# The FFN's output bias: from two TensorE matmuls per pass to an in-place GpSimd add on the residual

## What is computed

```
x = x + attn_a(layernorm(x))
x = x + ffn(layernorm(x))
x = x + attn_b(layernorm(x))
x = x + ffn(layernorm(x))
...
h = relu(x @ Wq1.T + b1)      # Wq1, Wq2: weights rounded to -1, 0, 1
out = h @ Wq2.T + b2
```

## Time and profile before

| | |
|---|---|
| median of three runs | 3095.37 us (3094.39 to 3095.38) |
| span of the profiled execution | 3093.2 us; it gives no other time of its own, so 2.2 us lie around the span |
| instructions | 79316 |
| matmul instructions | 27332, of which 128 at L446 |
| granted TensorE clock over the span | 0.988 of 2.4 GHz |

### The profile page before, as it was taken

The page is one execution under the profiler, slowest core; times in us unless marked ns, Lnnn a source line. Parts: engine busy times, 40 slices in busy tenths (PEclk is TensorE's granted clock), DMA queues, the critical chain, the costliest instruction groups (busy, mean ns, idle before and its releaser), DMA issues. The chain is left out here.

```text
span 3093.2 us, 79316 instructions
## 1 busy us (share of the span) xinstructions
PE 2935.6 (95%) x27332; PEld 2329.8 (75%) x27332; DVE 2363.1 (76%) x5980; ACT 1845.7 (60%) x3717; POOL 461.7 (15%) x1048
## 2 busy tenths in 40 slices
PE   5799999999999999999999999999999999999987
PEld 4677777777777777777777777777777777777765
DVE  5677788777788777788777788777788777888754
ACT  2356665566665566665566665566665566665565
POOL 4111111111111111111111111011111011111010
PEclk8999999999999999999999999999999999999998
DMA  2000000000000000000000000000000000000000
GB/s 65 8 11 17 16 16 3 14 16 16 16 16 3 14 16 16 16 16 3 14 16 16 16 16 3 14 16 16 16 16 3 14 16 16 16 16 3 15 11 17
DMA packets 42116, 44.86 MB, mean 15 GB/s; under 512 B 2640, under 2 KB 41424, under 8 KB 42064
## 3 DMA queue, kind: packets, MB, share of 16 engines
q1 hardware_dynamic: 42064, 44.20, 4.7%
HBM read 21.12 MB, written 16.78 MB: 12 GB/s over the span
## 5 line engine op out<-in xcount | busy, mean ns | idle before, releaser
L981 ACT ACTIVATE f_r<-HID,b1c 128x512 f32<-128x512 f32 x512 | 352.3, 688 | 501.0 <-PE HID L430 499.1
L450 PE MATMUL Y<-w2t,f_hh 128*128 128x256 f32 x2048 | 549.4, 301 | 4.8 <-DVE f_hl L1322 4.8
L450 PE MATMUL Y<-w2t,f_hl 128*128 128x256 f32 x2048 | 512.1, 283 | 0.0
L1322 DVE TENSOR_TENSOR f_hl<-f_r,f_hh 128x512 fp32r<-128x512 f32 x512 | 352.6, 689 | 127.9 <-ACT f_hh L982 119.6
L430 PE MATMUL HID<-ff_xh,w1t 128*128 128x512 f32 x1024 | 432.3, 422 | 4.6 <-DVE ff_xl L1314 4.6
L450 PEld LDWEIGHTS Y<-w2t,f_hh 128*128 128x128 f32 x2048 | 389.0, 190 | 47.9 <-issue 28.5
L430 PE MATMUL HID<-ff_xl,w1t 128*128 128x512 f32 x1024 | 406.9, 397 | 0.0
L450 PEld LDWEIGHTS Y<-w2t,f_hl 128*128 128x128 f32 x2048 | 391.0, 191 | 3.1
L982 ACT ACTIVATE f_hh<-HID,b1c 128x512 fp32r<-128x512 f32 x512 | 350.5, 685 | 0.0
L1428 DVE TENSOR_TENSOR a_s<-Q,cst 128x512 f32<-128x512 f32 x384 | 249.1, 684 | 52.1 <-PE Q L576 52.1
L1159 ACT ACTIVATE a_qz<-Q 128x512 f32<-128x512 f32 x512 | 280.0, 611 | 1.6 <-PE Q L780 1.6
(11 more groups left out here) (193 smaller groups left out, 7314.2 us busy)
## 6 DMA issues: line engine op xcount, KB each, us to landing
x<-in_x SPq DMA_DIRECT2D x32, 512.0 KB, 4.3
out<-x SPq DMA_DIRECT2D x32, 512.0 KB, 3.0
b_vm<-b_v SPq DMA_DIRECT2D x64, 96.0 KB, 2.1
x<-in_w SPq DMA_DIRECT2D x2, 512.0 KB, 4.0
a_s<-in_w_qkv SPq DMA_DIRECT2D x1, 768.0 KB, 5.0
ff_xn<-in_w SPq DMA_DIRECT2D x1, 512.0 KB, 6.7
f_r<-in_w SPq DMA_DIRECT2D x1, 512.0 KB, 7.0
cst<-in_const SPq DMA_DIRECT2D x1, 389.0 KB, 5.5
```

Source lines behind the costliest of these rows:

```text
L450: mm = pe.matmul(Y[t // 2][:, (t % 2) * D:(t % 2 + 1) * D], h[:, fb % 2, t * P:(t + 1) * P], w2t[:, fb, :], start=False, stop=(fb == FB - ...
L981: act.activation(f_r[:, fb % 2, :], banks[fb % 2][:], ACT.Relu, bias=b1c[:, fb:fb + 1]).then_inc(f_rr, 1)
L1322: dve.tensor_tensor(f_hl[:, fb % 2, :], f_r[:, fb % 2, :], f_hh[:, fb % 2, :], ALU.subtract).then_inc(f_lo, 1)
```

## The change

The bias is added to the residual tile itself, by POOL, once `normed` says that DVE has read all four tiles for the norm. `f_finish` gets one more wait, on the new semaphore. The two matmuls go, and with them their operands; the first product in each bank opens it.

```diff
-        b2f = sb("b2f", [4 * BR, D])
-        b2r = sb("b2r", [4 * BR, 2, D], F32R)
+        b2f = sb("b2f", [P, D])
...
-                    for j, y in enumerate(Y):
-
-                        rows = slice(2 * BR * j, 2 * BR * j + 2 * BR)
-                        pe.matmul(y[:], share[rows, :], b2r[rows].rearrange("p t n -> p (t n)"), start=True, stop=False,
-                                  skip_group_check=True)
                 for t in tiles:
                     for j, h in enumerate((f_hh, f_hl)):
                         mm = pe.matmul(Y[t // 2][:, (t % 2) * D:(t % 2 + 1) * D], h[:, fb % 2, t * P:(t + 1) * P],
-                                       w2t[:, fb, :], start=False, stop=(fb == FB - 1 and j == 1), skip_group_check=True)
+                                       w2t[:, fb, :], start=(fb == 0 and t % 2 == 0 and j == 0), stop=(fb == FB - 1 and j == 1),
+                                       skip_group_check=True)
...
                     dve.wait_ge(f_w2, (turn + 1) * FB)
+                    dve.wait_ge(f_biased, turn + 1)
...
+            def add_bias(turn, src):
+
+                pool.wait_ge(ff.normed, (turn + 1) * NT)
+                pool.tensor_tensor(src[:], src[:], b2f[:].unsqueeze(1).broadcast_to([P, NT, D]), ALU.add).then_inc(f_biased, 1)
```

DVE's three preparations of `b2r` and `share` go too. In POOL's order the add for `x3` stands at the head of `phase1`, before the norm of attention b. The add for `x1` stands in `phase2` behind `sines(3)`, before the norms for the next sequence:

```diff
                     sines(0)
                     sines(1)
                     own_rstd()
                     sines(2)
                     sines(3)
+                    own_bias()
                     next_rstd()
                     second_rstd()
```

More of the change, by code:

```diff
@@ L45 @@
 MASKED = -1e30
-BR = 32
 ROOT_SCALE = 0.375
@@ L117, in build @@
         b1c = sb("b1c", [P, FB])
-        b2f = sb("b2f", [4 * BR, D])
-        b2r = sb("b2r", [4 * BR, 2, D], F32R)
+        b2f = sb("b2f", [P, D])
         ones_f = sb("ones_f", [P, P])
-        share = sb("share", [4 * BR, P], F32R)
         gains = sb("gains", [P, H + KVH])
@@ L218, in build @@
         x_in, stored = sem("x_loaded"), sem("x_stored")
-        f_h, f_rr, f_act, f_lo, f_w2, f_out = (sem(n) for n in (
-            "f_hidden_ready", "f_relu_ready", "f_hi_ready", "f_lo_ready", "f_down_done", "f_added"))
+        f_h, f_rr, f_act, f_lo, f_w2, f_out, f_biased = (sem(n) for n in (
+            "f_hidden_ready", "f_relu_ready", "f_hi_ready", "f_lo_ready", "f_down_done", "f_added", "f_residual_biased"))
         (a_vp, a_v_s, a_kn, a_kt_s, a_qk, a_eq_s, a_rq_s, a_ph, a_qz_s, a_sc0, a_sc1, a_sc2, a_sc3, a_sm, a_u, a_st, a_o, a_ne, a_nt, a_dn,
@@ L327, in _ @@
             sp.dma_start(b1c[:], b1).then_inc(loaded, 16)
-            sp.dma_start(b2f[:], b2.partition_broadcast(4 * BR)).then_inc(loaded, 16)
+            sp.dma_start(b2f[:], b2.partition_broadcast(P)).then_inc(loaded, 16)
             sp.dma_start(mixc[:], mix).then_inc(loaded, 16)
@@ L1256, in prepare_rest @@
                     dve.tensor_scalar(mixed[:, i, :], st_wo[:, 0, :], mixc[:, i:i + 1], None, ALU.mult).then_inc(setup, 1)
-                dve.tensor_copy(b2r[:], b2f[:].unsqueeze(1).broadcast_to([4 * BR, 2, D])).then_inc(prepared, 1)
                 dve.wait_ge(setup, 4)
@@ L1269, in prepare_rest @@
                     dve.tensor_tensor(lo[:], src, hi[:], ALU.subtract).then_inc(prepared, 1)
-                dve.wait_ge(prepared, 6)
-                for low in (slice(BR, 2 * BR), slice(3 * BR, 4 * BR)):
-                    dve.tensor_tensor(b2r[low], b2f[low].unsqueeze(1).broadcast_to([BR, 2, D]), b2r[low], ALU.subtract).then_inc(prepared, 1)
                 dve.wait_ge(setup_pe, 1)
@@ L1285, in prepare_rest @@
                 dve.tensor_copy(qmask[:], C["qodd"]).then_inc(prepared, 1)
-                dve.tensor_scalar(share[:], ones_f[0:4 * BR, :], 1.0 / BR, None, ALU.mult).then_inc(prepared, 1)
                 dve.tensor_scalar(gains[:, 0:H], gains[:, 0:H], HD ** -0.5 * ROOT_SCALE, None, ALU.mult).then_inc(prepared, 1)
@@ L1796, in norm_rstd, with own_bias @@
                 root(n.tmp, n.chain, turn * 5, n.rstd[:], n.ready)
+            def add_bias(turn, src):
+                pool.wait_ge(ff.normed, (turn + 1) * NT)
+                pool.tensor_tensor(src[:], src[:], b2f[:].unsqueeze(1).broadcast_to([P, NT, D]), ALU.add).then_inc(f_biased, 1)
             def program(guarded):
                 def phase1(s):
+                    def own_bias():
+                        if s.c is not None:
+                            add_bias(second_turn(s.c), x3)
                     def next_rstd():
@@ L1822, in own_rstd, with own_bias @@
                             norm_rstd(ff, first_turn(s.a))
+                    def own_bias():
+                        if s.a is not None:
+                            add_bias(first_turn(s.a), x1)
                     def next_rstd():
```

## The result

The changed kernel takes 3172.9 us (3170.0 to 3174.0, 5 runs) against 3095.4 us; the ratio is 1.025, 95% interval 1.0239 to 1.0261. That is 77.6 us slower, 16 us less than the 3189 of the forecast and inside its range. The span of its profiled execution is 3171.1 us, 77.9 more than before, and the mean granted clock 0.982 against 0.988.

What follows compares the result with a forecast made beforehand. PE is fullest, but waits for ACT and DVE absorb the removed matmuls; POOL's add holding DVE's read path stalls PE. 3093.2 + 68 + 6 + 22 - 2 = 3187, plus 2 around the span: 3189 us, range 3120 to 3225.

Steps and rivals of the forecast that it cites:

- the hold of DVE's read path by the add: Phase2, x1 add: POOL holds DVE's L1622 for 2.2 us, delaying PE's turn_qk(1, 0), in 31 steps: 68 us.
- The pairs: Removed bias matmuls: 0 gained in phase2 and phase1; with FFNs that run alone and preparations at DVE's start, -2 us.
- POOL waits for the running instruction, then goes ahead of the next.: Who gets the read path when POOL and DVE both want it, read from sines; applied to the x1 add behind L1620.
- the victim in the prediction: L1622, DVE's two-SBUF-input b_ks instruction in phase2, expected to be held 2.2 us and recorded with some 2.4 instead of 0.28.
- the signs that the text named for being wrong: L1622 keeps its 0.28 us, PE finds other slack in phase2, or the add takes much less than 2.1 us.
- the one thing on which the prediction said it turns: Phase2: whether L1622 ends 0.8 us after the last normed tile, as now, or 3.0.
- the rule that the prediction took from the Trainium skill: VectorE and GpSimd share an exclusive port lock, kept for the whole instruction: hold 2.4 us, phase2 term 74 us instead of 68.
- The clock: PE's stalls in phase2 lower its granted clock: 0.7 us a step in 31 steps, 22 us, between 0 and 53.
- Phase1: The x3 add, behind phi(1), holds low(6) about 2.0 us; 0.2 us left in 30 steps: 6 us, bounds 0 to 60.
- DVE goes first, POOL fits in behind: Rival: POOL's add runs while norm_lo and f_finish read PSUM, holding nothing; 3080 us, faster; chance 0.10, same 0.04.
- The hold is short: Rival: the add reads ahead and lets DVE go after 1.3 us; 34 us, no loss of clock, 3127 us; chance 0.07.

Runs made afterwards that it cites:

- run 1: The changed kernel without POOL's add and DVE's wait for it, only the bias matmuls and their preparations removed: 3089.3 us, ratio 0.9979 to the kernel before.
- run 2: The kernel before with POOL's adds and DVE's wait put in, bias matmuls kept: 3178.8 us, ratio 1.0273.
- run 5: The changed kernel with one more DVE wait in phase2, for its own norm_qk(1) result ahead of low(7): 3195.4 us, measured once.
- run 10: The changed kernel with one more DVE wait inside stack_lo(1) in phase2, ahead of the b_ks subtraction: 3214.3 us, ratio 1.0393 to the kernel before.
- Run 3: The changed kernel with both adds issued later, x1 behind norm_qk(2), x3 behind low(7): 3089.3 us, ratio 0.9982 to the kernel before.
- run 6: The changed kernel with POOL's two-input add replaced by a one-input operation (x times 1 plus 0): 3104.1 us, ratio 1.0034 to the kernel before.
- run 9: The changed kernel with DVE's phase2 order changed, norm_lo and f_finish ahead of norm_qk(2): 3135.4 us, ratio 1.0130 to the kernel before.

## Why the prediction was right, and where it was not

**Right:** that the hold of DVE's read path by the add decides, its length (about 2 us, nearly to POOL's end), that a pair is worth 0.28 us to PE in phase2, which is lost again at `up(2)`, where PE waits for ACT (8.04 us from `up(0)` to `up(2)` in the changed kernel, 8.02 before; the window in the earlier trace rows begins 1.35 us behind the start of `up(0)`), and that PE has no slack there. The pairs were put at -2 us. They give 6 us by the medians of runs 1 and 2, still a fifth of the 30.5 us.

**The step that failed:** "POOL waits for the running instruction, then goes ahead of the next." It was read from the earlier trace rows, and holds there: L1567 stands behind L1322 without a gap (530.75, before 530.83), and in all 31 steps with such a pair POOL goes ahead of it. But L1567 reads one SBUF tile, and the victim in the prediction reads two. Against L1609, L1611, L1310 and L1595, which follow each other with no gap, POOL waited through all of them, 1.6 us, and got in where DVE itself waited; so its record has 3.98 us and not the 2.3 to 2.5 that the prediction expected. So L1622 (now L1611) kept its 0.28 us, the wait for `b_ks` did not grow, and `norm_qk(2)`, `norm_lo` and `up(0)` were late in its place. A kept 0.28 us was one of the signs that the text named for being wrong, and L1611 ends 548.46 - 547.66 = 0.80 us behind the last normed tile, as before: the one thing on which the prediction said it turns came out against it. Runs 5 and 10 show that a gap alone moves the hold to whichever instruction stands behind it. On the length of the hold, the rule that the prediction took from the Trainium skill ("SBUF — State Buffer", section "SBUF: two separate sides": the first keeps the pair for its whole instruction) comes close: the held L1604, 0.49 us long, ends 0.34 us behind POOL, so it was let go some 0.15 us before POOL's end.

**Why the sum came close all the same.** In part this is luck: the instruction that was held in place of the predicted one happened to stand ahead of another wait without slack. Two terms were sized by the wrong victim. The hold cost 1.78 us a step instead of 2.2, because a hold of 2.01 us of `norm_qk(2)` reaches `up(0)` as 6.25 - 4.40 = 1.85 us, and the step as 1.78. The clock cost 10 us instead of 22, because the clock fell after a PE wait of 1.78 us in 8 of 29 steps, and after the 2.29 us of run 10 in 24. With the predicted victim the hold came to the predicted size (2.1 us a step), but the clock to 12 x 1.3 + 12 x 2.3, some 43 us: there the forecast would have been 25 us too low.

**Phase1** went as described, with `low(6)` behind a gap and held for 2.0 us:

```profile
587.74 0.69 DVE L1401 SCALAR_TENSOR_TENSOR a_kT<-a_eq,a_relu 128x512 f32<-128x512 f32 x1
588.54 2.68 DVE L1310 TENSOR_TENSOR f_hl<-f_r,f_hh 128x512 fp32r<-128x512 f32 x1
```

What is left of it at the end of the second part is 0.43 us and not 0.2: 12 us instead of 6.

**The rivals.** "DVE goes first, POOL fits in behind" was half true in its first words and still gave a loss: DVE did go first, four times, but then came a gap ahead of one more instruction with two SBUF inputs, not the PSUM reads. Run 3 makes that rival real, at 3089 us; its price of 3080 took half of the pairs' time as gained, and they gave 6 of 30.5 us. "The hold is short" is what run 6 makes, by a shorter operation.

## What to carry to other kernels

In this kernel, work moved to GpSimd was free where VectorE read PSUM meanwhile. Price such work by the VectorE instructions with two SBUF inputs that run beside it, and look for the first gap in VectorE's queue to see which of them it will hold. Two semaphore waits that place the adds were worth 84 us here, more than the whole change could gain. And before counting removed matmuls as time, find the next two waits behind them: the second takes what the first gives back.

## What the runs showed that was not expected

- A waiting POOL instruction did not get in between DVE instructions with two SBUF inputs that follow each other without a gap; gaps of 0.1 to 0.2 us let it in, and so did, without a gap, a next instruction that reads PSUM (L1302 in run 9) or one SBUF tile (L1567 before). Its record then starts at the request: 3.98 us for work of 2.35. One step stands against it. In the first step with both attentions L1611 was held, though it is the same pair of instructions:

```profile
164.78 0.68 DVE L1609 TENSOR_TENSOR b_qs<-a_s,b_qs 128x512 fp32r<-128x512 f32 x1
165.39 2.44 DVE L1611 TENSOR_TENSOR b_ks<-a_s,b_ks 128x128 fp32r<-128x128 f32 x1
```

It is so in runs 2, 5 and 6 too. In that step no `low(7)` stands behind the pair; whether this is why POOL won there, and in none of the following steps, stays open.

- The clock: the same wait of 1.78 us is followed by a fall in 8 of 29 steps and by none in the others, so the price of one stall can't be read from one step. What sets the 8 apart is not shown.
